# Conditioned mixture-of-experts layer on one core: routing in halves, batched one-hot matrices, y rows turned back, and three shared steps instead of four ahead of the expert rounds

## The reference, cut to what is computed

```python
w = weights[conditions]                       # 32 of 200 matrices, each 32x32
y = einsum('bct,bcd->bdt', x, w)              # x: 32 x 32 x 256; 1024 tokens of 256
xt = y.reshape(1024, 256)
probs = softmax(xt @ w_router)                # 16 experts
top_w, top_i = top_k(probs, 4); top_w /= top_w.sum()
g = silu(einsum('td,edh->teh', xt, we1)) * einsum('td,edh->teh', xt, we3)   # H = 128
moe_out = einsum('teh,ehd->td', g * cw[:, :, None], we2)
shared = silu(xt @ ws1) * (xt @ ws3) @ ws2    # hidden 512
out = x + shared / 5 + moe_out * (4 / 5)
```

## Time and profile before

| | |
|---|---|
| three runs without a profile | 146.83, 150.36, 150.56 us (median 150.36) |
| the profiled execution, its own time | 146.87 us |
| its span, first to last instruction | 145.0 us |
| mean granted TensorE clock | 0.996 of full |
| PE, DVE, ACT, POOL busy | 92%, 71%, 54%, 46% of the span |

### The profile page before, as it was taken

One profiled execution on the slowest core, in us unless ns is written; L12 is line 12 of the kernel. 1 busy time (PEld: TensorE's weight loads), 2 busy tenths in 40 slices (PEclk: granted clock), 3 DMA queues, 4 the chain that ended last, 5 costly groups with the idle time before them and its releaser, 6 DMA issues.

```text
span 145.0 us, 2785 instructions
## 1 busy us (share of the span) xinstructions
PE 133.6 (92%) x786; PEld 112.0 (77%) x786; DVE 103.3 (71%) x290; ACT 78.9 (54%) x193; POOL 66.3 (46%) x79
## 2 busy tenths in 40 slices
PE   5999999989798999999999999899999999999470
PEld 2347997778487788999898889798999888888350
DVE  1301879998828999877879887887888653066992
ACT  4003637999404986677586777447945321107900
POOL 0700000002765687778776566577777777000000
PEclk9999999999999999999999999999999999999998
DMA  2823898989952232365437322122222222399924
GB/s 43 288 60 80 239 255 291 341 250 285 368 189 75 77 98 83 112 183 181 152 107 204 124 101 92 66 113 109 109 106 87 101 109 112 85 392 411 374 77 145
DMA packets 17549, 24.18 MB, mean 167 GB/s; under 512 B 3424, under 2 KB 14304, under 8 KB 17408
## 3 DMA queue, kind: packets, MB, share of 16 engines
q1 hardware_dynamic: 13440, 14.23, 30.1%
q0 software_dynamic: 3120, 8.52, 16.6%
q10 hardware_dynamic: 976, 1.26, 2.6%
HBM read 17.58 MB, written 6.42 MB: 166 GB/s over the span
## 4 chain that ended last, share of the span: by engine, by line
PE 61%; DVE 21%; DMA 7%; issue 5%; ACT 3%; DVEq 1%; ACTq 0%
PE up_ps L1004 17%; PE down_ps L1022 11%; PE down_ps L920 8%; PE gate_ps L907 5%; PE up_ps L907 4%; PE up_ps L998 4%; PE gate_ps L957 4%; PE down_ps L982 3%; PE down_ps L862 2%; DMA itok_rows<-in_itok_B 2%; DMA g<-in_L_cond_weights,cond_idx 2%; DVE g L632 2%; ACT w_hi L468 2%; DVE raw L805 2%; DVE x_lo L764 2%
## 5 line engine op out<-in xcount | busy, mean ns | idle before, releaser
L444 POOL DMA_INDIRECT result<-store_t,back_i x32 | 31.3, 979 | 12.9 <-issue 6.7
L437 POOL DMA_INDIRECT xt<-y_of,token_i x16 | 16.3, 1019 | 35.0 <-DVE token_i L716 28.1
L798 DVE SCALAR_TENSOR_TENSOR store_t<-down_ps,valid,store_t 128x256 f32 x47 | 21.7, 461 | 8.7 <-DVE store_t L798 5.8
L1004 PE MATMUL up_ps<-w_hi,x_hi 128*128 x78 | 23.8, 305 | 1.1 <-DVE x_lo L764 0.9
L1022 PE MATMUL down_ps<-w,gt 128*128 x94 | 24.5, 381 | 0.0
L1004 PE MATMUL up_ps<-w_lo,x_hi 128*128 x78 | 22.1, 283 | 0.0
L1004 PE MATMUL up_ps<-w_hi,x_lo 128*128 x78 | 22.0, 282 | 0.0
L437 POOL DMA_INDIRECT raw<-y_of,token_i x16 | 15.8, 985 | 4.9 <-issue 4.0
L1022 PEld LDWEIGHTS down_ps<-w,gt 128*128 128x128 f32 x94 | 16.0, 190 | 1.7 <-issue 0.5
L1004 PEld LDWEIGHTS up_ps<-w_hi,x_hi 128*128 128x128 f32 x78 | 14.8, 190 | 2.5 <-issue 2.4
L764 DVE TENSOR_TENSOR x_lo<-store_t,x_hi 128x256 fp32r<-128x256 f32 x39 | 14.8, 421 | 0.6 <-ACT x_hi L536 0.3
(11 more groups left out here) (156 smaller groups left out, 260.0 us busy)
## 6 DMA issues: line engine op xcount, KB each, us to landing
raw<-in_L_ffn_we SPq DMA_DIRECT2D x30, 128.0 KB, 3.3
w<-in_L_ffn_we SPq DMA_DIRECT2D x4, 512.0 KB, 6.4
w_lo<-result SPq DMA_DIRECT2D x4, 512.0 KB, 6.7
raw<-result SPq DMA_DIRECT2D x4, 512.0 KB, 7.0
acc<-in_x SPq DMA_DIRECT2D x2, 512.0 KB, 4.6
y_of<-store_t ACTq DMA_DIRECT2D x1, 1024.0 KB, 6.0
out<-acc SPq DMA_DIRECT2D x3, 256.0 KB, 2.2
xt<-in_L_ffn_ws SPq DMA_DIRECT2D x4, 128.0 KB, 2.7
```

The lines of the kernel that those rows point to most:

```text
L437: pool.indirect_dma_start(rows_of(p)[:, j % 2, :], None, y_of, bass.IndirectOffsetOnAxis(ap=token_i[:, j:j + 1], axis=0),).then_inc(tile_i ...
L444: pool.indirect_dma_start(result, bass.IndirectOffsetOnAxis(ap=back_i[:, j:j + 1], axis=0), merged[:, j, :], None,).then_inc(result_out[j ...
L798: dve.scalar_tensor_tensor(out=into, in0=out_ps[n % 2][:, h, :], scalar=valid[:, it:it + 1], in1=into, op0=ALU.mult, op1=ALU.add).then_inc ...
L1004: last = pe.matmul(gu_ps[b][:, h, :], (x_hi, x_lo)[a][:, b, h, k * P:(k + 1) * P], pair_of(w, experts[h], k), start=(m == 0), stop=(m == 3 ...
```

## The change

It has six parts.

- **Halves.** The four largest logits, their indices and the 0/1 choices (`pick`) are made for the first half of the tokens, then `low(0)`, then the same for the second half. `top_d` moves behind the mask.
- **Batched one-hots.** `row_hot` is built with 4 instructions of 1024 elements in place of 32 of 128, with all operands bf16; `tile_hot` likewise from bf16. `dest_hot` has two parts instead of three, one by ACT (1 instruction), one by DVE (1 instruction of 1024 elements). The layouts are turned: the matmuls of `choices` now read `row_hot` at a step of 8 elements and `dest_hot` at a step of 32, and have 64 columns in place of 96. DVE first computes `back_i`, then `token_i` from it by a shift.
- **y's rows turned back.** ACT copies y from PSUM to SBUF in fp32 (4 instructions), PE transposes that (16 transposes of 128 columns) in place of the 8 matmuls of 256 columns (16 instructions).
- **Second matrices later.** SP waits for the gathers of the first four tiles before it issues the four transfers of `w_2`; PE's wait for them moves to the first L1035.
- **Three shared steps ahead.** `STEPS` is 3. Unit 1 is used for one half ahead and for the other at the very end, for which its weights are loaded and converted again (unit number AGAIN, loaded behind the 14th turned pair, converted in round 16). Five steps come after the rounds.
- **Tail order.** The gates of steps 3 and 4 stand in the last four pairs, one half (3 matmuls) each; behind the rounds ups, gates and downs are interleaved anew. `gate_up(0, 0, [0])` stands ahead of `ranks`, `down(1, [0])` ahead of `item_rows`.

The diff, cut to its core:

```diff
-    STEPS = 2 * FRONT
+    STEPS = 2 * FRONT - 1
+    AGAIN = UNITS + NSH - FRONT
+    LATE_UNITS = {UNITS: 2, UNITS + 1: 3, AGAIN: 1}
+    STEP_UNITS = [0, 0, 1, UNITS, UNITS, UNITS + 1, UNITS + 1, AGAIN]
-    LOAD_BEHIND = {7: UNITS - 2, 8: UNITS - 1, 10: UNITS, 12: UNITS + 1}
+    LOAD_BEHIND = {7: UNITS - 2, 8: UNITS - 1, 10: UNITS, 12: UNITS + 1, 14: AGAIN}
+            for j in range(2 * RING - 2):
+                sp.wait_ge(tile_in[j], 16)
             for q in range(4):
                 sp.dma_start(w_2[:, e, :], we2[e].rearrange("e h d -> h e d")).then_inc(w_2_in, 16)
...
-            high(0)
-            high(1)
+            for h in range(2):
+                for k in range(KD):
+                    act.wait_ge(y_lo_done, KD * h + k + 1)
+                    act.activation(y_f[:, k, h * HALF:(h + 1) * HALF], y_ps[h][k][:, :], ACT.Copy).then_inc(y_f_done, 1)
+                high(h)
...
                 for t in range(TH * h, TH * h + TH):
                     step(dve.max(top_v[:, t, :], lg[:, t, :]))
+                dve.wait_ge(route, done[0])
+                for t in range(TH * h, TH * h + TH):
+                    step(dve.max_index(top_i[:, t, :], top_v[:, t, :], lg[:, t, :]))
+                if h == 0:
+                    low(0)
+                dve.wait_ge(route, done[0])
+                step(dve.tensor_tensor(pick[:, r, :, :], ..., ALU.is_equal))
...
-            dve.tensor_tensor(tile_hot, repeat(count_i[:, 0:TILES], TK), spread(tile_i[:, :], TILES), ALU.is_equal)
-            chain(dve.tensor_copy(row_f[:, :], row_i[:, :]))
+            step(dve.tensor_copy(tile_f, tile_i[:, :]))
+            chain(dve.tensor_copy(row_f, row_i[:, :]))
+            dve.tensor_tensor(tile_hot, count_tile, repeat(tile_f, TILES), ALU.is_equal)
+            dve.wait_ge(tile_hot_done, 1)
+            dve.tensor_tensor(dest_hot[:, 1, :, :], tile_hot, repeat(count_n, TILES), ALU.mult)
...
             def rows_hot(c):
-                for n in range(TT * c, TT * c + TT):
-                    dve.tensor_scalar(row_hot[:, n, :], count_r[:, :], row_f[:, n:n + 1], None, ALU.is_equal)
+                dve.tensor_tensor(row_hot[:, c, :, :], count_row, repeat(row_f[:, TT * c:TT * c + TT], P), ALU.is_equal)
...
-                    last = pe.matmul(row_ps[j][:, i * D:(i + 1) * D], cond_bd[:, 2 * j + i, :], acc[:, 2 * j + i, :], start=True, stop=True)
+                    t = 2 * j + i
+                    for k in range(KD):
+                        last = pe.transpose(row_ps[j][:, i * D + k * P:i * D + (k + 1) * P], y_f[:, k, t * P:(t + 1) * P], ident[:, :])
...
-                    last = pe.matmul(dest_ps..., row_hot[:, n, :], dest_hot[:, n, :, :]...)
+                    last = pe.matmul(dest_ps..., row_hot[:, c, :, i], dest_hot[:, :, :, n]...)
...
             gate_up(2, 0)
             choices()
             gate_up(2, 1)
-            gate_up(3, 0)
-            gate_up(3, 1)
+            down(1, [0])
             item_rows()
-            down(1, [0])
             down(2)
             pe.wait_ge(items_done, 4)
             down(1, [1])
...
-            down(3)
...
             gate_up(STEPS, 1)
-            gate_up(STEPS + 1, 0)
             gate_up(STEPS + 1, 1)
+            gate_up(STEPS + 2, 0)
             down(STEPS)
+            gate_up(STEPS + 2, 1)
+            gate_up(STEPS + 3, 0)
+            down(STEPS + 1)
+            gate_up(STEPS + 3, 1)
+            gate_up(STEPS + 4, 0)
+            down(STEPS + 2)
+            gate_up(STEPS + 4, 1)
+            down(STEPS + 3)
+            down(STEPS + 4)
```

More of the change, by code:

```diff
@@ L158, in adaln_ffn @@
         ones = small[:, 576:576 + P // 2].bitcast(BF16)
-        count_r = small[:, 640:640 + P // 2].bitcast(BF16)
+        count_n = small[:, 640:640 + TK // 2].bitcast(BF16)
         later = early(8, 2)
         tile_i, row_i = (later[:, k * TK:(k + 1) * TK].bitcast(I32) for k in range(2))
-        row_f, token_f = (later[:, k * TK:(k + 1) * TK] for k in range(2, 4))
+        row_f, tile_f = (later[:, k * TK:(k + 1) * TK].bitcast(BF16)[:, 0:TK] for k in range(2, 4))
+        place_f = early(10, 1)[:, 0:TK]
         parts = later[:, 128:128 + 4 * E].rearrange("p (m e) -> p m e", e=E)
@@ L183, in adaln_ffn @@
         four = raw[:, 5:13, :].rearrange("p (t e) (k d) -> p t (e k) d", t=4, d=D)
-        two = [w_lo[:, 2 * i + 2:2 * i + 4, :].rearrange("p e (k d) -> p (e k) d", d=D).bitcast(F32) for i in range(4)]
+        two = [w_lo[:, 2 * i + 3:2 * i + 5, :].rearrange("p e (k d) -> p (e k) d", d=D).bitcast(F32) for i in range(4)]
         back_in = two[0:2] + [four[:, t, :, :] for t in range(4)] + two[2:4]
@@ L237, in adaln_ffn @@
         items_done = sem("items_done")
-        w_in = [sem(f"w_in{n}") for n in range(E + NSH)]
+        w_in = [sem(f"w_in{n}") for n in range(AGAIN + 1)]
         w_2_in = sem("w_2_in")
@@ L492, in _ @@
                 high(n)
+            act.wait_ge(diff_done, 1)
+            act.activation(top_e[:, :, :], top_d[:, :, :], ACT.Exp).then_inc(exp_done, 1)
             def shared_silu(s):
@@ L506, in _ @@
                     act.wait_ge(tile_hot_done, 1)
[L507 to L513 removed]
+                    act.activation(dest_hot[:, 0, :, :], tile_hot, ACT.Copy, scale=part[:, 0:1]).then_inc(dest_hot_done, 1)
                 for n in HI_G[s]:
@@ L611, in _ @@
             dve.wait_ge(const_done, 9)
-            step(dve.tensor_copy(count_r[:, :], count_w))
+            step(dve.tensor_copy(count_row, spread(count_w, TT)))
+            step(dve.tensor_copy(count_tile, spread(count_w[:, 0:TILES], TK)))
+            step(dve.tensor_copy(count_n, count_w[:, 0:TK]))
             step(dve.tensor_copy(sums[:, 0, :], ones_e[:, :]))
@@ L643, in _ @@
                     step(dve.max(top_v[:, t, :], lg[:, t, :]))
-            dve.wait_ge(route, done[0])
-            dve.tensor_tensor(top_d[:, :, :], top_v[:, :, 0:TOP_K], top_v[:, :, 0:1].to_broadcast((P, TT, TOP_K)), ALU.subtract).then_inc(diff_done, 1)
-            for t in range(TT):
-                step(dve.max_index(top_i[:, t, :], top_v[:, t, :], lg[:, t, :]))
-            dve.wait_ge(route, done[0])
-            chain(dve.tensor_tensor(pick[:, :, :, :], count_i[:, 0:E].bitcast(U32).rearrange("p (a b e) -> p a b e", a=1, b=1).to_broadcast((P, TT, TOP_K, E)),
-                                    top_i[:, :, 0:TOP_K].rearrange("p t (k a) -> p t k a", a=1).to_broadcast((P, TT, TOP_K, E)), ALU.is_equal))
+                dve.wait_ge(route, done[0])
[4 more added lines that the diff above has]
+                dve.wait_ge(route, done[0])
+                step(dve.tensor_tensor(pick[:, r, :, :], count_i[:, 0:E].bitcast(U32).rearrange("p (a b e) -> p a b e", a=1, b=1).to_broadcast((P, TH, TOP_K, E)),
+                                       top_i[:, r, 0:TOP_K].rearrange("p t (k a) -> p t k a", a=1).to_broadcast((P, TH, TOP_K, E)), ALU.is_equal))
+            dve.wait_ge(route, done[0])
             with nc.allow_low_precision(reason="0 and 1 are exact in bfloat16"):
@@ L924, in down @@
                     last.then_inc(down_done, 1)
+            pe.wait_ge(dve_lo, 1)
+            gate_up(0, 0, [0])
             ranks()
-            for s in range(2):
-                pe.wait_ge(dve_lo, 1)
-                if s == 1:
-                    pe.wait_ge(row_out, 4)
-                gate_up(s, 0)
-                gate_up(s, 1)
+            gate_up(0, 0, [1])
+            gate_up(0, 1)
+            pe.wait_ge(row_out, 4)
+            gate_up(1, 0)
+            gate_up(1, 1)
             pe.wait_ge(w_2_in, 16)
```

113 lines of the change are left out of this document (52 added, 61 removed).

## The result

| | before | after |
|---|---|---|
| median of the runs | 148.70 us (4 runs, 146.83 to 150.56) | 155.21 us (4 runs, 154.62 to 157.75) |
| ratio, 95% interval | | 1.054 [1.047, 1.061] |
| the profiled execution, its own time | 146.87 us | 157.75 us |
| its span, mean granted clock | 145.0 us, 0.996 | 156.0 us, 0.954 |

The changed kernel is slower by over 4%, where 1.4% was forecast, and outside the range of 146.3 to 152.2. The ratio leaves disturbed runs out, so it is not the quotient of the two medians. Every run of the changed kernel had a mean clock between 0.943 and 0.958.

The account below looks back on a forecast made before the run. TensorE's work was taken to set the time outside the end, with 2.03 us of idle time in the front. 146.87 + 4.51 - 2.65 + 0.1 (late second matrices) + 0.1 (unit 1 again) = 148.9 us, range 146.3 to 152.2.

Parts of the forecast that it names:

- The moved step: Tail: step 3's 12 gate and up matmuls (2.78) and its `down` (1.73) move behind the rounds, +4.51 us.
- What the front gives back: From the logits to the expert rounds: VectorE's chain and TensorE's work shorten, so the rounds run 2.65 us earlier.
- 0.4 were the batched one-hots': Front, `tile_hot` to `gated(0)`: two casts and three instructions at 0.68 us replace 2.66 us, so `gated(0)` starts 0.4 earlier.
- The halves: Front, indices and `pick` by halves: 0.97 us saved, 0.65 lost to a late start; slots net 0.2 us earlier.
- `choices` ... I take no change: L904, 32 matmuls at 1.39 us: fewer columns might save 0.4, the new layout might cost; taken as unchanged.
- The rival: L904: strided loads or streams as slow as fp32, 3.5 us not 1.39, +2.1, total 151.0 us; chance 0.2.
- I charge 0.1, range 0 to 0.7: Late second matrices share the DMA engines with the gathers of pairs 3 and 4; charged 0.1 us.
- The landing of `w_2`: Second matrices land by 50.4 us at the latest, asked for at 51.6: no cost, 1.2 us of cover.
- PE's clock falls in the 3 us of idle time: Rival, ahead of the items: at 1.2 GHz downs and transposes double, about 2 us reach the rounds, total 151; chance 0.06.
- buy idle time: Front: y's rows by transposes save 1.8 us but end before the mask, so they only add idle time.
- A gain of 0.6 us at `gated(0)`: Front: one-hots (0.4) and halves (0.2) together start `gated(0)` 0.6 us earlier; the items were then put 0.65 earlier.
- half way: Range's lower end, 146.3 us: half way to the best case of 143.0, where the front shrinks more (rival, chance 0.17).

Follow-up runs that it names:

- e6: The changed kernel with the old one-hots and `w_2` issued early (halves, turned rows, three steps ahead left); median 151.95 us, 4 runs.
- e7: The kernel before with the batched one-hots and their strided contraction alone; median 150.17 us, ratio 1.009 to before.
- e10: The kernel before with `row_hot` alone in the new layout, so `choices` loads its stationary operand at a step of 8 elements; 153.18 us, 1 run.
- e13: e8 with the four transfers of `w_2` issued late, as in the changed kernel; median 148.85 us, ratio 1.004 to before.
- e1: The changed kernel with `w_2` issued early, as before; median 153.92 us, ratio 1.041 to before.
- e15: The kernel of e6 run again, beside e16 on the same chip; median 153.39 us, 6 runs, ratio 1.035 to before.
- e16: The kernel of e6 with ten unread matmuls filling TensorE's idle time ahead of the items; median 150.34 us, 6 runs, ratio 1.018 to before.
- e14: The changed kernel with ten unread matmuls put ahead of the spread of the table of items; median 155.36 us, ratio 1.047 to before.
- e4: The kernel before with y copied out in fp32 and its rows turned back by transposes; median 147.33 us, ratio 0.995 to before.
- e8: The kernel before with halves and turned rows only (four steps ahead, old one-hots, `w_2` early); median 146.99 us, ratio 0.993 to before.
- e5: The changed kernel with the old one-hots, their layout and contraction; median 153.97 us, ratio 1.038 to before.
- e12: e8 with `row_hot` built by 4 instructions of 1024 elements in the old layout; median 146.76 us, ratio 0.995 to before.
- e2: The changed kernel with y's rows computed by matmuls, as before, in place of transposes; median 157.22 us, ratio 1.066 to before.
- e11: The kernel before with `dest_hot` alone turned, so `choices` streams its moving operand at a step of 32 elements; 163.69 us, 1 run.
- e3: The changed kernel with both `w_2` issued early and y's rows by matmul; median 155.83 us, ratio 1.053 to before.

## Why the prediction was wrong

**The moved step: right.** +4.51 forecast, 4.52 read from e6. VectorE's chain behind the last product kept its length (10.05 us to the end of its last addition, in before, after and e6 alike); e6's span ends 13.75 us behind that product's start and not 13.35, and this 0.4 lies behind VectorE.

**What the front gives back: mis-sized by 0.8 us, where the clock stays full.** Forecast were items at 38.85, 3.0 us of idle time ahead of them, the first expert matmul at 44.6 and the second at 46.9; e6 has 39.13, 2.84, 44.92 and 47.19. The first matmul with a second matrix comes 2.0 us earlier than before (52.15 against 54.16), and the rounds end 1.82 earlier (117.94 less the 1.40 of added gates, against 118.36), not 2.65. So 146.87 + 4.52 - 1.82 = 149.57, and 149.81 was measured. Of the 2.65, 0.4 were the batched one-hots', which e6 lacks. That part was right: from the slots to `gated(0)` stand 2.54 us in after (28.07 to 30.61) and 2.95 in e6 (25.32 to 28.27), and `tile_hot` took 0.69 us where 0.68 was forecast. The halves gave `gated(0)` 0.4 us by themselves (28.27 in e6 against 28.70), not 0.2.

**Failed: "`choices` ... I take no change".** L904 took 3.71 in the chain, 2.3 us more, and the token number came at 38.98 in after, 4.9 us behind e6's 34.09. Of these, 2.3 stand ahead of `choices` (34.63 against 32.30): the ranks came 2.75 later (25.66 against 22.91), behind 6 us at 1.2 GHz, less the 0.4 of the one-hots. Another 2.3 are `choices`, and 0.2 the instruction added ahead of the token number. The rival had place and price (3.5 us, +2.1) and got 0.2. It deserved more: the earlier trace rows show a step of 8 bytes and say nothing of 16 or 64. By the rule of the Trainium skill, "SBUF — State Buffer", section "SBUF: two separate sides" (the note on cachelines), these steps had to cost something, though it gives no price. e7 (3.85 us) and e10 (loads 67 to 72 ns apart, not 43) agree. The same note counts a step of 8 bf16 elements, which is that of the stationary operand, as free; e10 shows that here it was not.

**Failed: "I charge 0.1, range 0 to 0.7" for the late second matrices.** Taken by themselves 1.85 us (e13), 1.3 in the changed kernel (e1). The landing of `w_2` was worked out and forecast to cost nothing, and it cost nothing: issued at 46.5 to 48.0 us, landed 10.2 us later at most, asked for at 60.7. But what 2 MB on the same engines does to the gathers beside it was put at a tenth. It was there to be read: a share of 0.81 in the earlier trace rows with the transfers of `w_2` early, and a gather of 4.8 us among others of 3.0 in the earlier trace rows, when they overlapped only in part.

**Failed: the rival "PE's clock falls in the 3 us of idle time" had 0.06.** The idle time was forecast to 0.2 us, the place to 0.3, the price at 2 us; measured, with the old one-hots and early `w_2`, the clock fell in most executions (six of ten by their times), and filling the idle time gave back 3.0 us (e15 against e16). For the changed kernel as a whole this price is not shown: its one profile has a full clock there, and the filler gave it nothing (e14). The argument against it was a full clock through 1.03 us of idle time, which shows nothing for 3. The forecast also rested on one execution at 0.996 while two of three times stood 3.5 us above it: another level was already in the table, and the forecast did not ask whether a change that takes work out of the front would meet it more often. After had no execution above a mean clock of 0.958.

**Failed: the rows of y "buy idle time".** They bought 1.2 us of median (e4). As far as times and clocks show, they made executions with a low clock behind the logits cheaper and not the fast ones faster.

**Small slips.** A gain of 0.6 us at `gated(0)` became 0.65 further on, and "half way" was worked out as 146 and used as 146.3. Neither changes anything.

**The sum in medians.** From before (148.5): turned rows -1.2 (e4), halves -0.3 (e8), three steps ahead +6.3 (e8 to the ten runs of e6 and e15, 153.3), of which 3.0 the clock and 3.4 the step less the front's gain; `w_2` late +0.7 (e5), batched one-hots +1.2 (after): 155.2. The last two are not clear of the spread one by one; together, 1.9 us from e15 to after, they are. Put into kernels with four steps ahead they cost more, 1.85 (e13) and 1.7 (e7). That falls of the clock overlap and are not paid twice would explain it, but is not shown.

**Better than both, though by under 1% in the ratio to before:** e8, 146.99 us, and e12, 146.76: four steps ahead, `w_2` early, plain layouts, halves and turned rows.

## What to carry to other kernels

Work that is taken out of a stretch in which TensorE waits may be what kept its clock up: count the idle time that the change opens, and if a filler of dead matmuls brings time back, the clock was the cost. Batch small instructions by all means, but look at who reads the result, and at what step; what VectorE saved off the path, TensorE paid for on it. A transfer that is moved off one place lands in another: ask which short gathers it now meets.

## What the runs showed of the hardware

- A 128x64 bf16 matmul with its load took 116 to 120 ns with operands at steps of 16 bytes (stationary) and 64 bytes (moving), a 128x96 one without steps 43 ns; with the stationary step alone the loads came 67 to 72 ns apart.
- A bf16 write at a step of 16 bytes took VectorE 0.32 us for 128 elements against 0.175; ScalarE's write of 1024 at a step of 64 bytes 4.89 us against 1.14.
- VectorE took 0.69 us for 1024 bf16 elements with an operand repeated along an outer axis, and 1.22 with it repeated along the innermost.
- Behind 2.8 us of idle time the granted clock went to 1.2 GHz for about 7 us (e15: 0.51 in 40.5 to 47 us), and nearly doubled the twelve `down` instructions, 5.49 against 2.86 us. By the times, six of that kernel's ten executions had it in full; in the profiles of e6 and after the same idle time left the clock at 1.00.
- The clock also fell at the end of or just behind 3.85 us of strided `choices`, with TensorE counted as busy (e7: 0.50 in 40 to 42 us; e1 and e14 alike), in three of six profiles.
- In the profiles of after, e2, e4, e5, e7 to e11 and e14 to e16 the clock also fell to 1.2 GHz behind the logits (after: 0.50 in 19 to 25 us, with TensorE busy for 6.00 of 6.00 us); in those of before, e1, e3, e6, e12 and e13 it did not. What decides it from one execution to the next was not found.
